# Decoder layer on one core: the projections of the next batch may start during the last products of the batch ahead

## The reference, cut to what matters

```python
def block_a(x):          # gated delta rule, 4 key heads, 8 value heads of 128, then a mixture of 8 experts
    qkvz = zrms(x) @ W_qkvz                       # 256 -> q 512, k 512, v 1024, z 1024
    beta, g = sigmoid(b), -exp(A_log) * softplus(a + dt_bias)   # b, a = zrms(x) @ W_ba
    q, k, v = split(silu(causal_dwconv(q_k_v, conv_w)))         # 4 taps along the sequence
    q, k = l2norm(q) * DK ** -0.5, l2norm(k)
    # per step t:  S = S * exp(g_t);  S += k_t (beta_t (v_t - k_t S));  o_t = q_t S
    core = rms(o) * gate_norm_w * silu(z)
    h = x + core @ W_out
    return h + sum(route_e * (silu(y @ Wg_e) * (y @ Wu_e)) @ Wd_e for e in top2)   # y = zrms(h)
x = layernorm(x + block_a(x))
x = layernorm(x + cross_attention(x, ctx))        # 16 heads of 16, 128 keys
y = x + gelu(x @ W_cols + b) * weights @ proj_w + proj_b      # 16 columns of 64, the best one kept
x = layernorm(layernorm(y) * ln_g + ln_b)
```

## Time and profile before

| | us |
|---|---|
| median of three timed runs | 2474.32 (2469.8 to 2476.02) |
| the profiled execution | 2487.57 |
| its span, first to last instruction | 2485.8 |
| TensorE busy | 2284.7 (92%) |
| VectorE busy | 1717.6 (69%) |
| ScalarE busy | 1396.9 (56%) |
| GpSimd busy | 808.5 (33%) |

### The profile page before, as it was taken

The page is one execution under the profiler, slowest core; times in us unless marked ns, Lnnn a source line. Parts: engine busy times, 40 slices in busy tenths (PEclk is TensorE's granted clock), DMA queues, the critical chain, the costliest instruction groups (busy, mean ns, idle before and its releaser), DMA issues.

```text
span 2485.8 us, 82876 instructions
## 1 busy us (share of the span) xinstructions
PE 2284.7 (92%) x34026; PEld 1924.9 (77%) x34026; DVE 1717.6 (69%) x5322; ACT 1396.9 (56%) x4326; POOL 808.5 (33%) x1771
## 2 busy tenths in 40 slices
PE   5899999999999999999999999999999999999986
PEld 4678887778787777787777787777787777787775
DVE  4476777766777666777767777767777667777753
ACT  3465455665555664555665555665555665555642
POOL 2233323333324332233333233333233333333321
PEclk8899999999999999999999999999999999999996
DMA  5000000000000000000000000000000000000000
GB/s 207 6 2 7 9 9 9 9 2 9 9 9 8 4 6 9 9 9 8 4 6 9 9 9 9 4 6 9 9 9 8 4 7 9 9 9 8 7 4 5
DMA packets 25064, 30.75 MB, mean 12 GB/s; under 512 B 8528, under 2 KB 21856, under 8 KB 23920
## 3 DMA queue, kind: packets, MB, share of 16 engines
q1 hardware_dynamic: 24688, 25.46, 3.2%
HBM read 21.25 MB, written 4.19 MB: 10 GB/s over the span
## 4 chain that ended last, share of the span: by engine, by line
PE 54%; ACT 27%; DVE 14%; issue 3%; POOL 1%; DVEq 0%; POOLq 0%
PE bank_b L640 9%; PE bank_a L456 6%; PE bank_b L648 4%; ACT acc L810 4%; PE bank_a L577 3%; PE bank_a L528 3%; PE bank_b L669 3%; DVE diag L1040 3%; PE bank_a L585 3%; PE bank_a L568 3%; PE bank_b L601 3%; DVE y1p L1134 3%; ACT prob L947 2%; PE bank_a L538 2%; ACT ypad L807 2%
## 5 line engine op out<-in xcount | busy, mean ns | idle before, releaser
L1004 DVE SCALAR_TENSOR_TENSOR acc<-ypad,convw,acc 128x128 f32<-128x128 f32 x1536 | 450.1, 364 | 180.3 <-ACT acc L810 180.3
L456 PE MATMUL bank_a<-xnT,wqkvz 128*128 128x128 f32 x2048 | 272.0, 294 | 0.0
L456 PEld LDWEIGHTS bank_a<-xnT,wqkvz 128*128 128x128 f32 x2048 | 261.9, 209 | 0.0
L905 ACT ACTIVATE y1T<-bank_b 128x256 f32<-128x256 f32 x32 | 12.3, 385 | 347.2 <-PE bank_b L662 347.2
L1411 POOL TENSOR_SCALAR lnv<-mv 128x1 f32<-128x1 f32 x128 | 24.6, 192 | 486.5 <-DVE mv L1095 483.9
L917 ACT ACTIVATE prob<-bank_b,nmax 128x128 f32<-128x128 f32 x512 | 181.3, 385 | 2.2 <-DVE nmax L1154 1.8
L1369 POOL TENSOR_TENSOR ostat<-ostat 128x4 f32<-128x4 f32 x64 | 12.9, 202 | 505.2 <-ACT gseg L871 505.2
L528 PEld LDWEIGHTS bank_a<-zblk,kkT 32*32 32x32 f32 x8192 | 93.4, 106 | 75.6 <-issue 71.5
L810 ACT ACTIVATE acc<-bank_a,convw 128x128 f32<-128x128 f32 x512 | 147.3, 388 | 0.0
L528 PE MATMUL bank_a<-zblk,kkT 32*32 32x32 f32 x8192 | 115.1, 195 | 33.1 <-DVE zblk L1048 21.3
L1152 DVE TENSOR_REDUCE smax<-bank_b 128x4 f32<-128x512 f32 x128 | 87.7, 685 | 68.4 <-PE bank_b L679 68.4
(11 more groups left out here) (244 smaller groups left out, 5957.3 us busy)
## 6 DMA issues: line engine op xcount, KB each, us to landing
xin<-in_x_dram SPq DMA_DIRECT2D x32, 128.0 KB, 2.0
cin<-in_ctx_dram SPq DMA_DIRECT2D x32, 128.0 KB, 2.1
out_dram<-yout SPq DMA_DIRECT2D x32, 128.0 KB, 2.0
wqkvz<-in_wqkvz_dram SPq DMA_DIRECT2D x6, 512.0 KB, 6.3
...
wu<-in_wu_dram SPq DMA_DIRECT2D x1, 1024.0 KB, 13.2
...
```

The lines of the kernel that those rows point to most:

```text
L456: last = mm(A[bank][:, b * P:(b + 1) * P], wqkvz[:, c, o:o + P], xnT[:, c, :], start=(c == 0), stop=(c == KC - 1))
L1004: stt(acc[:, c, :], ypad[:, c, k:k + P], convw[:, c, k:k + 1], acc[:, c, :], ALU.mult, ALU.add).then_inc(conv.sem, 1)
```

## The change

The four lists are written anew. On PE `a_xT` now stands behind `a_w1` (before: behind `c_xo`), `a_ba` and `a_qkv0` ahead of `c_pT3` and `a_o0`, `a_qkv1` ahead of `c_pv` and `a_o1`, which belong to the batch ahead. The banks of the qkv groups are exchanged: group 0 goes to bank 3, group 1 to bank 0, group 2 to bank 2, group 3 to bank 1; the z halves go to banks 0 and 3. Waits are added so that a bank is free of the batch ahead: `a_xT` for the first w subtraction, group 0 for the second, groups 2 and 3 for `a_core1` and `a_core0`, ACT's z silu for the `a_core` that reads `zs`. Waits on `tap_last` and `zs_ok` are exchanged to fit the banks. `szT` lies in the decay buffer instead of `acc`. Steps are moved in the lists of the other engines too; since the point at which the lists begin has moved, some steps have a lag of one more and stand at the head instead of the end. No instruction is added or taken out.

```diff
@@ -109,24 +109,24 @@
 
 
 ORDER = dict(
-    pe="a_lb10@1 a_la11@1 b_router@2 b_gu0@2 b_gu1@2 b_gu2@2 b_gu3@2 a_la20@1 a_lb11@1 b_dn0@2 a_la21@1 "
-       "a_lb20@1 b_dn1@2 a_la30@1 a_lb21@1 b_k@2 a_la31@1 a_lb30@1 b_y1T@2 a_lb31@1 b_q@2 a_pa@1 a_pb@1 c_s "
-       "a_vT1@1 a_mt@1 a_sz0@1 c_pT0 a_w0@1 a_sz1@1 a_o0@1 a_w1@1 c_pT1 a_o1@1 c_pT2 c_pT3 c_R c_pv c_xo "
-       "a_xT a_ba a_qkv0 a_qkv1 c_y2T a_qkv2 a_z0 a_z1 c_h a_kk a_qkv3 c_lg c_c0 a_ss c_c1 c_wT a_st a_dec0 "
-       "c_spread a_dec1 c_pj0 b_oT0 b_oT1 c_pj1 b_w0 a_la00 a_la01 b_w1 a_lb00 b_cT a_qk a_vT0 a_lb01 a_la10 "
-       "b_v b_x2T".split(),
-    act="b_cT@2 b_x2T@2 b_rl@2 b_sg0@2 b_sg1@2 b_rt@2 b_y1T@2 a_mix3@1 a_zf@1 b_q@2 a_zo@1 c_exp0 a_mt@1 "
-       "a_sz0@1 c_exp1 c_exp2 a_sz1@1 a_o0@1 c_exp3 a_o1@1 c_pT0 c_pT1 c_R a_sum a_xT a_ba a_qkv0 a_qkv1 "
-       "a_ln c_y2T a_z0 a_mix0 a_mix1 c_h a_qkv2 a_sq c_lt a_qkv3 a_st c_c0 c_te c_wT a_seg c_c1 a_dec0 "
-       "a_dec1 a_z1 b_oT0 a_mix2 b_oT1 b_sum".split(),
-    dve="b_v@2 a_lb10@1 b_top@2 a_la11@1 a_conv32@1 a_score@1 b_act0@2 b_act1@2 a_la20@1 a_lb11@1 b_ys0@2 "
-       "a_la21@1 a_lb20@1 b_ys1@2 a_lb21@1 a_la30@1 b_y1@2 a_la31@1 a_lb30@1 a_lb31@1 a_u0@1 b_k@2 a_pa@1 "
-       "c_max0 c_max1 a_u1@1 c_max2 c_max3 a_w0@1 a_w1@1 c_pT0 c_rec c_pT1 a_core0@1 c_ao a_core1@1 a_xn "
-       "c_sum2 c_y2 a_conv00 a_conv01 a_conv02 a_conv10 a_conv11 a_conv12 a_conv20 c_lb a_conv21 c_route "
-       "a_conv22 c_weight a_ss c_gc0 c_gc1 a_conv30 a_lower a_init a_la00 a_la01 c_y4@3 c_sum3 b_hid a_lb00 "
-       "c_y3 b_x2 a_la10 a_lb01 a_conv31".split(),
-    pool="b_ln0@2 a_osc0@1 a_osc1@1 a_x c_ln3@3 b_y1b@2 c_ln1 a_ga c_rx a_g c_sig b_mask a_sc a_rq c_y2b c_ln2 "
-       "b_rs b_rd b_xh a_xr b_rt".split(),
+    pe="a_la10@1 a_la11@1 b_router@2 b_gu0@2 b_gu1@2 a_lb10@1 b_gu2@2 b_gu3@2 a_lb11@1 a_la20@1 b_dn0@2 "
+       "a_lb20@1 a_la21@1 b_dn1@2 a_lb21@1 b_k@2 a_la30@1 a_la31@1 a_vT0@1 b_y1T@2 a_lb30@1 a_lb31@1 b_q@2 "
+       "a_pa@1 a_vT1@1 a_pb@1 c_s a_mt@1 a_sz0@1 a_sz1@1 c_pT0 a_w0@1 a_w1@1 a_xT c_pT1 c_pT2 a_ba a_qkv0 "
+       "c_pT3 a_o0@1 c_R a_qkv1 c_pv a_o1@1 c_xo a_z0 a_z1 a_qkv2 c_y2T a_qkv3 c_h c_c0 c_lg a_dec0 c_c1 "
+       "c_wT a_ss c_spread a_st a_kk a_dec1 c_pj0 b_oT0 c_pj1 b_oT1 b_w0 b_w1 a_la00 a_la01 b_cT a_qk b_v "
+       "a_lb00 a_lb01 b_x2T".split(),
+    act="b_oT0@2 b_oT1@2 a_mix2@1 b_sum@2 b_cT@2 b_x2T@2 b_sg0@2 b_rl@2 b_rt@2 b_sg1@2 a_sum a_mix3@1 b_y1T@2 "
+       "a_zf@1 b_q@2 a_zo@1 c_exp0 a_mt@1 c_exp1 c_exp2 a_xT c_exp3 a_sz0@1 c_pT0 a_ba c_pT1 a_sz1@1 a_qkv0 "
+       "a_o0@1 c_R a_qkv1 a_o1@1 a_ln a_mix0 a_z0 a_seg a_z1 c_y2T a_mix1 a_qkv2 c_h a_sq c_lt a_qkv3 c_c0 "
+       "c_wT a_st c_c1 c_te a_dec0 a_dec1".split(),
+    dve="a_lb01@1 b_v@2 a_la10@1 a_conv31@1 a_conv32@1 c_y4@3 b_top@2 a_la11@1 a_lb10@1 a_score@1 b_act0@2 "
+       "b_act1@2 a_lb11@1 a_la20@1 b_ys0@2 a_la21@1 a_lb20@1 b_ys1@2 a_lb21@1 a_la30@1 b_y1@2 a_la31@1 "
+       "a_u0@1 a_lb30@1 a_lb31@1 b_k@2 a_pa@1 c_max0 a_u1@1 a_xn c_max1 c_max2 c_max3 a_w0@1 a_w1@1 c_pT0 "
+       "c_rec c_pT1 a_conv00 a_conv01 c_ao a_conv02 a_conv10 c_sum2 a_core0@1 a_core1@1 a_conv11 c_y2 "
+       "a_conv12 a_conv20 c_lb a_conv21 c_route c_gc0 a_ss a_conv22 c_weight c_gc1 a_lower a_init c_sum3 "
+       "a_conv30 b_hid a_la00 c_y3 a_la01 b_x2 a_lb00".split(),
+    pool="b_mask@2 b_rs@2 c_ln3@3 b_xh@2 b_rd@2 a_xr@1 b_rt@2 b_ln0@2 b_y1b@2 a_x a_ga a_osc0@1 a_osc1@1 c_ln1 "
+       "a_g c_rx c_sig a_sc c_y2b c_ln2 a_rq".split(),
 )
 
 
@@ -220,7 +220,7 @@
         diagT, zinit = xblk, ablk
         zfull = sb("zfull", [P, HV, P])
 
-        szT = acc[:, 0:HV, :]
+        szT = decay
         carryT = gseg[0:64, :, 0:64]
         junk_o = gseg
         ostat = sb("ostat", [P, 7, HV])
@@ -296,7 +296,7 @@
         Bk = [ctx.enter_context(nc.psum_tensor(f"bank_b{i}", [P, 512], F32)) for i in range(4)]
 
         DOWN = (1, 1, 2, 2, 3, 3, 0, 0)
-        GROUPS = ((2, HK), (1, 0), (3, 2 * HK), (0, 3 * HK))
+        GROUPS = ((3, HK), (0, 0), (2, 2 * HK), (1, 3 * HK))
         A_LEVEL = (A[0], A[3])
         TOP, BOT = slice(0, 64), slice(64, P)
         PAIRS = ((slice(0, BLK), slice(BLK, 2 * BLK)), (slice(2 * BLK, 3 * BLK), slice(3 * BLK, P)))
@@ -440,6 +440,8 @@
 
             def a_xT(n):
                 pe.wait_ge(*x_norm(n))
+                if not first(n):
+                    pe.wait_ge(*w_ok(n - 1, 1))
                 for c in range(KC):
                     last = tr(A[0][:, c * P:(c + 1) * P], xn[:, c * P:(c + 1) * P], ident)
                 last.then_inc(xnT_ps.sem, 1)
@@ -448,8 +450,10 @@
                 bank, block = GROUPS[g]
                 if first(n):
                     pe.wait_ge(wqkvz_in[block // 4].sem, 16)
-                if g == 3:
+                if g == 1:
                     pe.wait_ge(*ba_ok(n))
+                elif not first(n):
+                    pe.wait_ge(*(w_ok(n - 1, 2) if g == 0 else core_ok(n - 1, 4 - g)))
                 for b in range(4):
                     o = (block + b) * P
                     for c in range(KC):
@@ -463,7 +467,7 @@
                 pe.wait_ge(*tap_last(n, (8, 4)[half]))
                 for c in range(KC):
                     o = CONV_DIM + 512 * half
-                    last = mm(A[1 + half][:, :], xnT[:, c, :], wqkvz[:, c, o:o + 512],
+                    last = mm(A[(0, 3)[half]][:, :], xnT[:, c, :], wqkvz[:, c, o:o + 512],
                               start=(c == 0), stop=(c == KC - 1))
                 last.then_inc(z_ps.sem, 1)
 
@@ -474,7 +478,7 @@
                 last.then_inc(ba_ps.sem, 1)
 
             def a_ss(n):
-                pe.wait_ge(*tap_last(n, 12))
+                pe.wait_ge(*zs_ok(n, 2))
                 pe.wait_ge(*sq_ok(n))
                 for q in range(4):
                     last = mm(A[3][32 * q:32 * q + 32, 0:2 * P], ones[:, :], sqk[:, 2 * q:2 * q + 2, :], start=True, stop=True)
@@ -495,7 +499,7 @@
 
             def exponents(n, half):
                 if half == 0:
-                    pe.wait_ge(*tap_last(n, 16))
+                    pe.wait_ge(*zs_ok(n, 1))
                 else:
                     pe.wait_ge(*sse_ok(n))
                 bank = (0, 3)[half]
@@ -505,7 +509,7 @@
 
             def a_kk(n):
                 pe.wait_ge(*mixed_ok(n, 1))
-                pe.wait_ge(*zs_ok(n, 1))
+                pe.wait_ge(*tap_last(n, 16))
                 for h in range(HK):
                     k = mixed[:, HK + h, :]
                     last = mm(A[1][:, h * P:(h + 1) * P], k, k, start=True, stop=True)
@@ -513,7 +517,7 @@
 
             def a_qk(n):
                 pe.wait_ge(*mixed_ok(n, 2))
-                pe.wait_ge(*zs_ok(n, 2))
+                pe.wait_ge(*tap_last(n, 12))
                 for h in range(HK):
                     last = mm(A[2][:, h * P:(h + 1) * P], mixed[:, HK + h, :], mixed[:, h, :], start=True, stop=True)
                 last.then_inc(qk_ps.sem, 1)
@@ -812,7 +816,9 @@
 
             def zgate(n, half):
                 act.wait_ge(*z_ps(n, 1 + half))
-                fn(heads(zs, half), quad(A[1 + half]), ACT.Silu).then_inc(zs_ok.sem, 1)
+                if not first(n):
+                    act.wait_ge(*core_ok(n - 1, 1 + half))
+                fn(heads(zs, half), quad(A[(0, 3)[half]]), ACT.Silu).then_inc(zs_ok.sem, 1)
 
             def a_ba(n):
                 act.wait_ge(*ba_ps(n))
```

## The result

The changed kernel takes 2331.76 us (median of four runs, 2329.35 to 2340.02), the kernel before in the same runs 2473.1 (2469.8 to 2476.02): a ratio of 0.9435, 95% interval 0.9407 to 0.9462. The profiled execution took 2329.89 us (span 2327.9), against 2487.57 (2485.8).

The account below looks back on a forecast made before the run. TensorE's work and gaps bound the kernel; gains of 4.7 less costs of 1.75 leave 3.0 us a trip, 90 over 30 trips; with 3 once and 11 of clock falls, 2474.3 becomes 2370 us, range 2335 to 2435.

Parts of the forecast that it names:

- What bounds the kernel now: TensorE, busy 94% of the steady stretch: only its work and gaps count; waits listed per trip, clock falls 24.1 us.
- The marks by place: Signs: which TensorE waits vanish, new ones at L456 (about 16 us) and L616 (3 to 25), clock 1.0 through qkv.
- The overlap: From b_q to the end of a_qkv1: seven waits get other work ahead of them, gaining 3.9 us a trip.
- walk to 21.1: Step-by-step timing from b_q: last step, now c_xo, gives way at 21.1 instead of 24.86, a gain of 3.8 us.
- What is late next: Behind init: b_hid and cT late, b_v waits 0.7 us a trip; small steps around c_y3 and a_la01 cost 0.45.
- `a_qkv2`'s 0.5: Before a_qkv2: bank 2 holds a_o1's result until VectorE's a_core1 reads it, costing 0.5 us a trip (0 to 1.0).
- The prologue: Second trip: xn waits no more on POOL, ending the single 4.9 us stop at a_xT; 3 us once.
- The clock: Falls to half clock at qkv end as TensorE no longer stops: 24 us off the profiled run, 11 off the median.
- B: At a_g: GpSimd waits out VectorE's conv run, making gates and later steps 2.5 us late a trip; 2445 us; chance 0.12.
- C: In the overlap: ScalarE's unbroken 14.4 us becomes the bound, only 0.6 a trip gained; 2456 to 2474 us; chance 0.04.
- D: From a_la00 to the router: stops make the clock fall in b_gu, 1.6 us each trip; 2418 us; chance 0.07.
- E: At a_g and a_sc: both GpSimd places blocked by conv, 3.6 us lost against 3.0 gained; 2489 us; chance 0.05.

Follow-up runs that it names:

- e4: Changed kernel with a_ba put right behind a_xT on TensorE, ahead of c_pT1 and c_pT2, bringing back one stop; 2361.75 us, 0.953 of the kernel before.
- e8: Changed kernel with a_vT1 put behind a_pb again on TensorE, bringing back one stop; 2353.57 us, 0.9506 of the kernel before.
- e6: Changed kernel with a_xT, a_ba, a_qkv0, a_qkv1 back behind c_xo, other engines' parts too, and a_qkv2 ahead of a_z0; 2429.27 us, 0.9811 of the kernel before.
- e13: Changed kernel with banks of qkv groups 2 and 3 exchanged, c_h, c_lb, c_route, b_cT queued earlier, and VectorE's a_la01 ahead of c_y3; 2333.28 us.
- e14: Like e13, with VectorE's b_x2 also ahead of c_y3, GpSimd's b_rs ahead of b_mask and c_y3's product in its own buffer; 2305.0 us.

## Why the prediction was right or wrong

**The bound and the direction** were right: TensorE's gaps were the bound, those that I listed in *What bounds the kernel now* went, and nothing took their place in that stretch. The marks by place came: no waits at `c_R`, `c_pv`, `c_xo` and `a_ba`, the new wait at L460 (forecast about 16 us, 17.1), the one on cT (3 to 25, 9.6), the clock at 1.0 through qkv; waits on exponentials stayed at 4.1 us in all. The mark by size did not: a trip of 70 to 71.5 was forecast and 69.53 came.

**The step that failed is the sum, in two of its terms; the first is *The overlap*, too small by 0.74 us a trip.** I took 3.9 us, from a walk to 21.1 and from 3.26 of idle plus 0.1 for each of seven stops. TensorE gets to `a_z0` at 20.12, where the usual trip of before was at 24.76, which is 4.64. From the start of the step ahead to the start of the stopped one, against the same step with another behind it and no stop, the seven cost about 4.35 us for 3.26 idle (`a_ba` 0.68 for 0.47, `c_pv` 0.62 for 0.43, `a_xT` 0.56 for 0.30). So the surcharge is about 0.15 a stop on the mean and up to 0.26. One stop put back alone showed 0.23 in e4 and none in e8, so this price is a mean and not a rule. The other 0.3 I can't give stop by stop; I take it to be in groups that follow one another in new pairs, which was not tried. The walk to 21.1 erred in the same way. For a step with a stop behind it, the rows of before have no distance to its neighbour without the stop, and its duration stood in; in the new rows `c_R` takes 0.22 (1467.03 to 1467.25) with a duration of 0.38, and `c_xo` 0.87 with 1.03. 0.74 x 30 = 22 us. ScalarE's holes of e6 were there in the kernel before too (3.02, 0.71 and 1.45 us ahead of `xnT`, `ba` and the first qkv copy), but TensorE waited no more than 0.9 us in the whole run for `y2T` behind them, so I count them as no part of this miss.

**The second is *What is late next* with the other terms behind `c_xo`, too dear by 0.72 us a trip.** Forecast 1.75 of cost and 0.8 of gain behind `c_xo`, 0.95 in all; measured 0.23 (49.18 to 49.41). `a_qkv2`'s 0.5 was right (0.49). `b_v` got 0.25 instead of 0.7: `b_hid` begins at 46.2, not 47.2 to 47.9, because everything ahead of it came a microsecond earlier, and GpSimd's scales with it. Behind it stood 0.15, not 0.45. The mechanism that I named there, `c_y3` ahead of `a_la01`, is the one that e13 and e14 found; I had priced it and not asked what it would hide. On the side of the gains, the steady stop before `a_la00` was 0.52 and not 0.6, and the new order ahead of `b_y1T` took the 0.23 before `a_la31` away, which I had left standing. 0.72 x 30 = 22 us.

**The prologue** gave 11 us, not 3. I counted the single 4.9 us stop at `a_xT` in the second trip as 3. The whole second trip came earlier with it: its `a_xT` starts at 71.2 instead of 80.1. The granted clock is 0.50 from 50 to 68 us in both kernels, and from 78 to 82 it is 0.60 in the kernel before and 1.00 in the changed one, so what the overlap saves there may count for more than in a steady trip; that was not tried by itself.

**The clock** was right: the 24.1 us of the profiled execution are gone. What I did not see are the 9.4 us of new irregular stops.

Together: 22 + 22 + 8 - 9 = 43 us more than forecast, less 2 because 2.95 a trip had been rounded up to 3.0; the profiled execution is 2370.6 less 2329.9, that is 40.7 below its sum, and the timed median 38 below its own.

**The rivals.** B did not come. Its condition was that `a_g` begins inside VectorE's conv steps. `a_g`'s first sum and what GpSimd does behind it, then VectorE, in the same trip:

```profile
1475.56 0.21 POOL L1355 TENSOR_TENSOR gate<-gate 128x8 f32<-128x8 f32 x1
1475.84 0.20 POOL L1357 TENSOR_TENSOR gate<-gate,negA 128x8 f32<-128x8 f32 x1
1476.26 3.05 POOL L1360 TENSOR_SCALAR gseg<-const,gate 128x128 f32<-128x128 f32 x4 [0.22 <-POOL gate L1357]
```

```profile
1473.91 2.13 DVE L1087 SCALAR_TENSOR_TENSOR u<-bank_a,ostat,zs 128x128 f32<-128x128 f32 x8
1475.95 1.17 DVE L1010 SCALAR_TENSOR_TENSOR acc<-ypad,convw,acc 128x128 f32<-128x128 f32 x4
1477.03 0.40 DVE L1105 TENSOR_SCALAR y<-y2p,mv,lnv 128x256 f32<-128x256 f32 x1
1477.36 1.28 DVE L1010 SCALAR_TENSOR_TENSOR acc<-ypad,convw,acc 128x128 f32<-128x128 f32 x4
```

VectorE is busy without a hole from 1473.91 to 1478.64. The sum begins inside that and takes 0.21, but it lies beside `a_core` steps (L1087), which read a PSUM bank, and is over 0.18 us before the first conv step (1475.95). I had 0.8 us between the two, and the sum escaped the conv steps by less, so it says little of my reading of the earlier trace rows, that a GpSimd step waits for the end of the whole run. The four scalings (L1360) say more: they begin at 1476.26, inside the conv steps that last to 1478.64, and end at 1479.31. Had the first of them waited for the end, the four, which took 2.37 alone before, would have ended near 1481. They took 3.05, a delay of a part of the run, so the reading does not hold in general. By the Trainium skill (SBUF — State Buffer, "Who interferes with whom") a VectorE instruction with two SBUF inputs contends with a GpSimd one that reads SBUF, and one with at most one SBUF input, outside the two-port modes, does not. These rows fit that better than my extension of it; the 2.21 us of before it doesn't explain, and no run here was made to. C did not come; in e6, where its requests begin later, ScalarE does set the trip, so it is close behind. D and E did not come: the clock stayed up in `b_gu`.
